# A token mixer with state-space and product-key layers on one NeuronCore: halved one-hot sums and a shifted TensorE plan

## What is computed

```
h = tok(x)                           # 4x4 pixels -> one token, attention of the mean over its 16 pixels
h = h + scan(layernorm(h))           # in-projection, selective scan both ways (128 channels, 16 states),
                                     # gate from the mean over the tokens, out-projection
h = h + ffn(layernorm(h))            # product-key memory, then causal attention

# ffn, for each of 8 heads:
sim      = q_pk . pk_keys            # two lists of 64 key scores per token and head
top 16 of each list, 256 sums of pairs, top 16 of these -> 16 rows of a table of 4096, softmax weights
k = sum_j score_j * keys_table[row_j]      ;  v = sum_j score_j * values_table[row_j]
sim = (x @ Wq) . k, causal, softmax, @ v, @ Wo
```

## Time and profile before

| | before |
|---|---|
| median of 3 runs | 11875.98 us (11864.46 to 11879.08) |
| profiled execution | 11876.72 us |
| its span | 11874.9 us |
| mean granted TensorE clock | 0.984 |
| busy: PE | 11007.4 us, 93% |
| busy: DVE | 10210.0 us, 86% |
| busy: POOL | 8452.9 us, 71% |
| busy: ACT | 7850.5 us, 66% |
| DMA | 1975.58 MB, mean 166 GB/s |

### The profile page before, as it was taken

One profiled execution on the slowest core, in us unless ns is written; L12 is line 12 of the kernel. 1 busy time (PEld: TensorE's weight loads), 2 busy tenths in 40 slices (PEclk: granted clock), 3 DMA queues, 4 the chain that ended last, 5 costly groups with the idle time before them and its releaser, 6 DMA issues.

```text
span 11874.9 us, 263894 instructions
## 1 busy us (share of the span) xinstructions
PE 11007.4 (93%) x70396; PEld 9141.7 (77%) x70396; DVE 10210.0 (86%) x42192; ACT 7850.5 (66%) x17926; POOL 8452.9 (71%) x8196
## 2 busy tenths in 40 slices
PE   3999999999999999999999999999999999999999
PEld 2777777777777777777777777777777777777777
DVE  6889898898898898888988988988988889889883
ACT  2666666666666666666666666666666666666665
POOL 0677777777777777777777777777777777777776
PEclk6999999999999999999999999999999999999999
DMA  2566565565565565665655655656656556556554
GB/s 63 155 175 176 161 175 168 168 178 162 169 181 160 173 177 161 175 172 164 177 166 171 178 160 172 181 158 175 175 163 175 171 166 176 162 171 180 158 169 136
DMA packets 1651836, 1975.58 MB, mean 166 GB/s; under 512 B 336238, under 2 KB 1125870, under 8 KB 1649902
## 3 DMA queue, kind: packets, MB, share of 16 engines
q1 hardware_dynamic: 1387950, 1418.48, 40.8%
q0 software_dynamic: 262144, 537.40, 16.8%
HBM read 1881.20 MB, written 73.40 MB: 165 GB/s over the span
## 4 chain that ended last, share of the span: by engine, by line
PE 54%; DVE 30%; issue 8%; ACT 5%; DMA 1%; DVEq 1%; POOL 0%; SPq 0%; ACTq 0%; POOLq 0%
PE bank L1008 15%; PE bank L1044 9%; DVE decay L1579 8%; PE bank L1031 6%; PE bank L1018 5%; DVE decay L1588 5%; PE bank L891 4%; ACT bank L1255 3%; DVE onehot L1804 3%; DVE apart L1709 3%; PE bank L972 2%; PE bank L995 2%; DVE decay L1590 2%; DVE row_f L1713 2%; PE bank L1060 2%
## 5 line engine op out<-in xcount | busy, mean ns | idle before, releaser
L819 POOL DMA_INDIRECT gath<-in_table_dram,rowsT x8192 | 8452.7, 1032 | 3394.1 <-issue 2468.8
L1008 PE MATMUL bank<-weight,rowtab 128*128 128x256 f32 x16384 | 4250.9, 381 | 0.0
L1262 ACT ACTIVATE weight<-bank 128x512 f32<-128x512 f32 x4096 | 2440.8, 596 | 2735.7 <-PE bank L1018 2703.2
L1008 PEld LDWEIGHTS bank<-weight,rowtab 128*128 128x128 f32 x16384 | 3109.6, 190 | 762.5 <-issue 20.2
L1255 ACT ACTIVATE bank<-bank,seventeen 128x512 f32<-128x512 f32 x4096 | 2711.1, 662 | 14.7 <-PE bank L1018 11.6
L1044 PEld LDWEIGHTS bank<-spread,gath 128*128 128x128 f32 x16384 | 2157.1, 192 | 148.6 <-issue 15.7
L1044 PE MATMUL bank<-spread,gath 128*128 128x96 f32 x16384 | 2112.5, 272 | 5.7 <-DMA gath<-in_table_dram,rowsT 5.7
L1031 PE MATMUL bank<-moving,pick_b 96*128 96x512 bf16 x4096 | 1580.1, 386 | 468.5 <-ACT bank L1255 399.3
L1018 PE MATMUL bank<-moving,pick_b 96*128 96x512 bf16 x4096 | 1557.7, 380 | 0.0
L1579 DVE TENSOR_TENSOR_SCAN decay<-decay,wide 128x256 f32<-128x256 f32 x2048 | 1238.0, 670 | 3.4
L1031 PEld LDWEIGHTS bank<-moving,pick_b 96*128 96x128 bf16 x4096 | 436.8, 107 | 908.6 <-ACT bank L1255 745.2
(11 more groups left out here) (268 smaller groups left out, 16966.3 us busy)
## 6 DMA issues: line engine op xcount, KB each, us to landing
rowtab<-in_tableD_dram SPq DMA_DIRECT2D x2048, 256.0 KB
wide<-states SPq DMA_DIRECT2D x512, 512.0 KB
moving<-keyspace SPq DMA_DIRECT2D x4096, 64.0 KB
gath<-in_table_dram,rowsT POOLq DMA_INDIRECT x8192
moving<-keyspace SPq DMA_DIRECT2D x4096, 32.0 KB
pix<-in_x_dram SPq DMA_DIRECT2D x504, 256.0 KB
keyspace<-split SPq DMA_DIRECT2D x256, 256.0 KB, 3.4
out_dram<-acc SPq DMA_DIRECT2D x64, 64.0 KB
```

The lines of the kernel that those rows point to most:

```text
L819: pool.indirect_dma_start(out=gath[:, u % RING, j, :], out_offset=None, in_=table, in_offset=bass.IndirectOffsetOnAxis(ap=rowsT[k][:, col: ...
L1008: mm(dense_ps[:, 0:TOK], rowtab[:, r, s % 2 * 2 + half, :], weight[s % 2][:, half * TOK:(half + 1) * TOK], start=(s % 16 == 0 and half == ...
L1262: ins = af(weight[s % 2][:], zd_ps[s % 2][:], ACT.Exp, scale=-1.0)
```

## The change

Each one-hot sum is cut in two. `S.E{n}` now does the 16 matmuls over onehot[0], a new step `S.H{n}` the 16 over onehot[1], each one adds one to a new semaphore hot_summed, and H stands one row behind E (H2 in row 0, across the end of the period). ACT's copy and DVE's one-hot steps wait for hot_summed where they waited for slot_step: the copy for both halves, e_n for the half that read its own buffer. Beside that, steps of PE's plan move by a row: kv10 from row 13 to 14, s3 from 15 to 16, a0.5 from 23 to 22, a0.6 from 25 to 24, xd and dt from 39 to 38, a2.5 from 39 to 40. ACT's plan follows in the copies of E2 and E0, a0.5, sc and xd. SP_ORDER, POOL's plan and DVE_ORDER stay as they are.

The core of the diff:

```diff
 PE_ORDER
-0 z63-1 o0+0 d62-1
+0 z63-1 o0+0 d62-1 S.H2+0
...
-6 z5+0 o6+0 d4+0 F.rf+2
+6 z5+0 o6+0 d4+0 F.rf+2 S.H3+0
...
-38 z37+0 o38+0 d36+0 S.A1+1
-39 z38+0 o39+0 d37+0 g2.3+0 a2.5+0 F.xd+2 F.dt+2
-40 z39+0 o40+0 d38+0
+38 z37+0 o38+0 d36+0 S.A1+1 F.xd+2 F.dt+2
+39 z38+0 o39+0 d37+0 g2.3+0
+40 z39+0 o40+0 d38+0 a2.5+0
 41 z40+0 o41+0 d39+0 g2.4+0 a2.6+0 S.E0+1
-42 z41+0 o42+0 d40+0 a3.0+0
+42 z41+0 o42+0 d40+0 a3.0+0 S.H0+1
...
-46 z45+0 o46+0 d44+0
+46 z45+0 o46+0 d44+0 S.H1+1
 ACT_ORDER
-0 w63-1 l0+0 k3-1 a5.5-1 F.sq2+2 F.sq3+2 S.E2+0
-1 w0+0 l1+0 K3-1
+0 w63-1 l0+0 k3-1 a5.5-1 F.sq2+2 F.sq3+2
+1 w0+0 l1+0 K3-1 S.E2+0
...
-40 w39+0 F.xd+2 l40+0 F.dt1+2
+40 w39+0 l40+0 F.xd+2 F.dt1+2
-42 w41+0 S.E0+1 l42+0 S.mi1+1
-43 w42+0 a3.0+0 l43+0
+42 w41+0 l42+0 S.mi1+1
+43 w42+0 a3.0+0 S.E0+1 l43+0
...
 second (PE)
-                if name[0] == "E":
-                    side = int(name[1])
+                if name[0] in "EH":
+                    side, t = int(name[1]), int(name[0] == "H")
+                    if t == 0:
...
+                    last.then_inc(hot_summed, 1)
 second (ACT), copy of E
-                    act.wait_ge(slot_step, seen(a, f"S.E{side}"))
+                    act.wait_ge(hot_summed, a * 8 + 2 * side + 2)
 second (DVE), step e
-                        wait(dve, slot_step, seen(a, f"S.E{n // 2 - 1}"))
+                        dve.wait_ge(hot_summed, a * 8 + n - 1)
```

More of the change, by code:

```diff
@@ L89 @@
 12 z11+0 o12+0 d10+0 a7.3-1
[L90 to L93, removed]
+13 z12+0 o13+0 d11+0 g0.6+0 S.s2+1 F.kv9+2
+14 z13+0 o14+0 d12+0 F.kv10+2 F.kv11+2
+15 z14+0 o15+0 d13+0 g0.7+0 a7.5-1
+16 z15+0 o16+0 d14+0 S.s3+1
 17 z16+0 d15+0 o17+0 g1.0+0 a7.6-1
@@ L98 @@
 21 z20+0 o21+0 d19+0 g1.2+0
[L99 to L102, removed]
+22 z21+0 o22+0 d20+0 a0.5+0
+23 z22+0 o23+0 d21+0 g1.3+0
+24 z23+0 o24+0 d22+0 a0.6+0
+25 z24+0 o25+0 d23+0 g1.4+0
 26 z25+0 o26+0 d24+0 a1.0+0
@@ L166 @@
 22 w21+0 l22+0
-23 w22+0 l23+0
-24 w23+0 F.sc+2 l24+0
-25 w24+0 a0.5+0 l25+0
+23 w22+0 l23+0 a0.5+0
+24 w23+0 l24+0 F.sc+2
+25 w24+0 l25+0
 26 w25+0 l26+0
@@ L631, in build @@
         slot_step = sem("slot_step")
+        hot_summed = sem("hot_summed")
         over_ready = sem("over_ready")
@@ L984, in second @@
                         pe.transpose(big_b[:, t * P:(t + 1) * P], moved[:, side, t, :], ident[:])
-                if name[0] == "E":
-                    side = int(name[1])
[L987 to L996, removed]
+                if name[0] in "EH":
+                    side, t = int(name[1]), int(name[0] == "H")
+                    if t == 0:
+                        if side == 1:
+                            pe.wait_ge(count_copied, a * 4 + 1)
+                        else:
+                            pe.wait_ge(rest_ready, a * 4 + (2, 0, 3, 4)[side])
+                    pe.wait_ge(onehot_ready, a * 8 + 2 * side + t + 1)
+                    hot = onehot[t][:].rearrange("p h k r -> p (h k) r")
+                    for r in range(TOPK):
+                        last = mm(big_b[:, t * P:(t + 1) * P], hot[:, :, r], down_b[:, r, :] if side == 1 else ident_b[:],
+                                  start=(r == 0), stop=(r == TOPK - 1))
+                    last.then_inc(hot_summed, 1)
             def product_part(b, s, half):
@@ L1792, in second @@
                     if n >= 2:
-                        wait(dve, slot_step, seen(a, f"S.E{n // 2 - 1}"))
+                        dve.wait_ge(hot_summed, a * 8 + n - 1)
                     elif not isinstance(a, int) or a > 0:
-                        wait(dve, slot_step, seen(a + (-1), "S.E3"))
+                        wait(dve, hot_summed, a * 8 + n - 1)
                     hot = onehot[n % 2]
```

## The result

The changed kernel takes **12000.4 us** (median of 4, 11994.4 to 12006.6); the kernel before took 11872.1 beside it. The ratio is 1.0108, 95% interval 1.0095 to 1.0121: **slower by 128 us**, 2.1 us per image. Slower was forecast, at 11919 and at most 11975. The place of the loss was right in one half and missed in the other.

What follows compares the result with a forecast made beforehand. PE was taken to bound rows 2 to 18, DVE rows 19 to 0. Per image -0.5 - 0.3 + 1.1 = +0.3, with the clock +0.7, x 60 = +42: 11919 us; eight in ten from 11830 to 11975.

Steps and rivals of the forecast that it cites:

- Two stretches, one of PE and one of DVE: Rows 2 to 18 (y to q0, 56.5 us) belong to PE, rows 19 to 0 (122.4 us) to DVE.
- E0 and H0, the term that decides: Rows 41 and 42: e3 waits for H0 behind a3.0, 1.1 us in every image, bounds 0.9 to 1.2.
- the stall without a clock: Rival: e3's wait costs time but no lower clock follows; +0.3 x 60 = +18, 11895 us; chance 0.24.
- The clock behind that hole: Row 42: PE's idle time before a3.0 grows from 0.63 to 2.2 us, lowering the clock; +0.4, bounds 0 and 1.0.
- E2 and H2, the clock in rows 1 and 2: A3 waits over a microsecond longer for ACT's copy: nothing, unless the clock falls, 1.5 each; bounds 0 and +30 us.
- a0.5 and a0.6: Rows 22 to 25, DVE's stretch: PE about 1.2 earlier; DVE takes 0.5 at h1 and perhaps 0.2 more; -0.7.
- xd and dt: Rows 38 to 40, DVE's stretch: the o for ACT's high part of A1 comes 0.45 later, so does DVE; +0.4.
- E3, kv10, s3: PE's stretch: E3 and H3 in rows 5 and 6 worth -0.2; kv10 and s3 in rows 13 to 16 save 0.3.
- The rival with the heavier clock: All of H0 at the lower level in each image, plus falls at row 1: +108 us, 11985; chance 0.14.
- the 24 of 28 that the prediction leaned on: Loop ends in the steady part followed by the lower clock level, used to expect a fall behind the 2.2 us hole.

Runs made afterwards that it cites:

- the last run: F.bk moved from row 3 to behind a6.3 in row 4, on the kernel with both repairs, xd and dt back in row 39, g0.1 in row 1: 11855.6 us.

## Why the prediction was right in one half and wrong in the other

- **Two stretches, one of PE and one of DVE: held.** Every wait added to DVE in the second came out (the stall whole, 0.47 of the rest's 0.55), and PE's saving in the first shows in every image whose clock stayed up. The 46.3 us given as DVE's busy time in the first stretch are PEld's column of the earlier trace rows; DVE's is 40.1, which makes the case stronger.
- **E0 and H0, the term that decides: held.** Forecast 1.1 with bounds of 0.9 and 1.2; measured 1.03 to 1.14 where the clock stayed up (mean 1.10), 1.3 to 2.3 where it fell. That move alone costs 68 us, 66 forecast for the stall without a clock; the agreement is partly luck, since 0.15 us per image of it lie in the first stretch.
- **The clock behind that hole: held.** Idle time 2.2 forecast, 2.30 to 2.42 measured; the clock fell in 26 of 58 images. +0.4 forecast, 0.23 measured: e3 waits 1.33 us in the mean of all images, 1.10 where the clock stays up. The Trainium skill, "TensorE: Matmul & The Clock Gate", section "Why this matters for your kernels", warns of idle gaps longer than any of these. Here 2.4 us, and 1.3 in row 1, were followed by the lower level, so the measurement decides against taking shorter gaps as safe.
- **E2 and H2, the clock in rows 1 and 2: the step that failed.** The prediction priced A3's later wait at nothing, "unless this idle time lowers the clock in PE's stretch", with 20 more falls and 30 us as the bound, and left that out of the sum. What came was a fall in rows 1 and 2 in 27 more images, ten of the 42 with two in a row: 0.94 us per image, 56 us. The mechanism was named and its price was right (1.5 us); the error was to leave it out of the sum, and to tie it to this one move. H2 in row 0 alone brought 36 falls and cost 39 us, but the moves of rows 5 to 16 alone brought 30 and lost their own 0.35 by it, and with E2 whole again the changed kernel kept 33 and gained only 28 us. So the 0.94 belongs to the moves together, and how it divides among them is not shown. The prediction also missed what is displaced: of the images behind a loop's end, 25 had a fall there or in rows 1 and 2 before and 24 after, but now 18 of them in rows 1 and 2, where they are paid, instead of 4.
- **a0.5 and a0.6: the second step that failed.** -0.7 was forecast, most of it DVE's wait at h1, which is 0.47 us in the mean before and after. q0 to h1 fell by 0.2 only (24.2 to 24.0 us). PE did come out of row 25 1.28 earlier, and gave 1.02 of it back at once, in row 26, ahead of a1.0, for the accumulation of a0.6:

```profile
4038.10 0.67 PE L1062 MATMUL bank<-xT,wq_ffn 128*128 128x256 f32 x2 [0.82 <-DVE acc L1840]
```

  This is the same wait as the one that decides in row 42, and it stands ahead of every stage 0; the prediction used it there and forgot it here. A lead of PE over DVE cannot pass an a-stage 0.
- **xd and dt: a little small.** +0.4 forecast, 0.55 measured as DVE's wait, 0.47 as the change of the stretch when they went back.
- **E3, kv10, s3: held.** -0.2 and -0.3 forecast; rows 5 and 6 took 0.21 less, rows 13 to 16 0.26. Some 0.15 of it went to a longer wait in row 18, which leaves about 0.35.

Put together by its own terms: -0.35 (for -0.5), +0.94 (for 0), -0.2 (for -0.7), +0.55 (for +0.4), +1.10 (for +1.1) and +0.23 (for +0.4) make +2.27 where +2.11 was measured and +0.7 forecast. The two terms that failed are 1.44 of it per image, 86 us, about the 81 between 11919 and 12000. The 0.16 that is left over lies in the second stretch and is given to no term. DVE also waits there for the DMA of wide (line 1588), which the prediction did not count: 0.22 us per image in the mean of the kernel before and of the changed one, and 0.07 in the run with H0 ahead of a3.0, so this does not explain it.

The rival with the heavier clock (11985) comes closest in its number, by luck, since its errors cancel: it took 1.0 for H0 at the lower level in each image, where 0.23 was measured, 30 us for row 1, where it was 56, and it kept the -0.7 of a0.5 and a0.6.

What stays open: why an idle time in one image is followed by the lower level and in the next, with the same rows, is not. Its length alone does not decide it. The idle time at the loop's end is 1.7 to 2.7 us before and 1.7 to 2.3 after, and the falls there went from 24 to 6 of 28, so the 24 of 28 that the prediction leaned on was no rate for an idle time of that length; and the last run idles 1.4 to 1.6 us in row 3 of every image, longer than A3 waits in the changed kernel, without a fall behind it. The runs show that filling idle time in row 1 with work takes most of the falls there away, and at which places a fall is paid; they don't show a condition from which the number of falls could be worked out.

## What to carry to other kernels

Where two engines hold different stretches of one period, sort the moves by stretch first; a saving in the other engine's stretch lasts only until the next wait that ties the two (here each a-stage 0), so name that wait. When a consumer is split off and put behind a step that waits, look at what releases that step: if it is the producer's own queue, the split closes a loop through both engines. Idle time that a move leaves on a matmul engine in the stretch it bounds can have a second price, the clock; put other work of the plan there, and where none fits, even repeated work paid here.

## What was not expected of the hardware

- Work without use made the kernel faster three times: 1.3 us per image more in the changed kernel (-30 us), 0.65 us more in two others (-19 and -39 us), each by fewer falls of TensorE's granted clock.
- In the run without xd and dt in row 38, 18 of the 29 images of even number had the clock at 1.2 GHz in rows 1 and 2, with a wait of 0.6 us ahead of F.g and others of 0.2 and 0.4 us near it; of the others, with 0.9 us in one piece ahead of F.g, 6 of 29 had it. With g0.1 moved in front of F.g there was none.
- Waits of 1.4 to 1.6 us in row 3 (F.bk a row later) were followed by no fall in any of 58 images.
- The number of falls changed less than their place: 41 before, 43 with the moves of rows 5 to 16 alone; that kernel lost its whole saving by having them in row 1 instead of at the loop's end. Across all runs the number does change: 74 in the changed kernel, 14 with g0.1 in row 1.
